# A GpSimd copy set behind the third expert addition, and an output product moved to another PSUM bank

## The reference

```
h = embed(x) * sqrt(192) + position
u = layernorm(h)
z, xBC, dt = split(rmsnorm(u) @ in_proj)        # 384, 512, 24 heads
xBC = silu(causal_conv(xBC, 4 taps) + conv_b)   # per channel, over time
state = exp(dt * A) * state + dt * x B^T        # per head, step by step
m = (state C + D x) * silu(z) @ out_proj        # the mixer
v = rmsnorm(m)
h = h + m + (silu(v @ w_gate) * (v @ w_up)) @ w_down
x = layernorm(h)
scores = sigmoid(x @ gate)                      # 8 experts in 4 groups of 2
cw = the 2 best experts of the 2 best groups, scores divided by their sum
h = h + shared expert(x) + sum over e of cw[e] * (silu(x @ w1[e]) * (x @ w3[e])) @ w2[e]
```

## Time and profile before

| | |
|---|---|
| median of 3 runs | 796.38 us (795.68 to 796.73) |
| the profiled execution | 796.69 us, of it the span of the trace 794.9 us |
| TensorE busy | 757.6 us (95%) |
| VectorE busy | 636.5 us (80%) |
| ScalarE busy | 546.8 us (69%) |
| GpSimd busy | 328.3 us (41%) |
| mean granted TensorE clock | 0.991 |

### The profile page before, as it was taken

How to read it: one execution, slowest core, us unless ns; L and a number is a source line. 1 busy time by engine, 2 the same in 40 slices (tenths; PEclk the granted TensorE clock), 3 DMA queues, 4 the chain that set the end, 5 groups by cost and what they waited for, 6 DMA issues and landing times.

```text
span 794.9 us, 23059 instructions
## 1 busy us (share of the span) xinstructions
PE 757.6 (95%) x7278; PEld 646.6 (81%) x7278; DVE 636.5 (80%) x1691; ACT 546.8 (69%) x1242; POOL 328.3 (41%) x478
## 2 busy tenths in 40 slices
PE   2679999999999999999999999999999999999897
PEld 1556788988888898888888888888988888888786
DVE  4699987879788787978878797887889788786745
ACT  4975777767777776777767677776767777675533
POOL 5355544433444443344344334434443443442222
PEclk9899999999999999999999999999999999999999
DMA  7420000000000000000000000000000000000000
GB/s 251 155 89 1 12 22 12 9 25 6 15 10 21 10 6 25 3 17 10 21 10 6 25 3 17 10 21 10 6 24 4 17 10 16 14 6 11 2 1 21
DMA packets 14923, 18.93 MB, mean 24 GB/s; under 512 B 4656, under 2 KB 13008, under 8 KB 14448
## 3 DMA queue, kind: packets, MB, share of 16 engines
q1 hardware_dynamic: 13264, 15.25, 6.0%
q0 software_dynamic: 1632, 3.34, 1.7%
HBM read 14.39 MB, written 4.19 MB: 23 GB/s over the span
## 4 chain that ended last, share of the span: by engine, by line
PE 87%; DVE 2%; issue 1%; ACT 1%; POOL 0%; DVEq 0%; POOLq 0%; ACTq 0%
PE bank L1554 40%; PE bank L1934 11%; PE bank L1862 8%; PE bank L1718 6%; PE bank L1707 5%; PE bank L1831 4%; PE bank L1818 3%; PE bank L1809 3%; PE bank L1795 2%; PE bank L1647 1%; PE bank L1652 1%; PE bank L1691 1%; DVE mr L1193 1%; PE bank L1901 0%; PE bank L1902 0%
## 5 line engine op out<-in xcount | busy, mean ns | idle before, releaser
L1193 DVE SCALAR_TENSOR_TENSOR mr<-er,gm 128x512 f32<-128x512 f32 x192 | 125.8, 692 | 4.1 <-ACT er L782 3.7
L782 ACT ACTIVATE er<-bank 128x512 f32<-128x512 f32 x192 | 106.0, 595 | 27.4 <-PE bank L1707 27.1
L1934 PE MATMUL bank<-w2t,w_raw 128*128 128x192 f32 x576 | 112.6, 327 | 0.4 <-DVE w_raw L1362 0.4
L872 ACT ACTIVATE sg<-bank 128x256 f32<-128x256 f32 x144 | 55.1, 382 | 61.8 <-PE bank L1554 50.9
L1132 DVE SCALAR_TENSOR_TENSOR xa<-xr,cw_,xa 128x256 f32<-128x256 f32 x192 | 92.4, 488 | 6.3 <-ACT xa L690 4.7
L1934 PEld LDWEIGHTS bank<-w2t,w_raw 128*128 128x128 f32 x576 | 91.0, 190 | 1.8 <-DVE w_raw L1455 0.7
L1554 PE MATMUL bank<-x_h,wt_lo 128*128 128x256 f16 x288 | 78.5, 273 | 0.0
L1554 PE MATMUL bank<-x_h,w_lo 128*128 128x256 f16 x288 | 78.5, 273 | 0.0
L1554 PE MATMUL bank<-x_l,w_hi 128*128 128x256 f16 x288 | 78.5, 272 | 0.0
L1554 PE MATMUL bank<-x_h,w_hi 128*128 128x256 f16 x288 | 78.4, 272 | 0.0
L1554 PE MATMUL bank<-x_h,wt_hi 128*128 128x256 f16 x288 | 78.4, 272 | 0.0
(11 more groups left out here) (239 smaller groups left out, 2197.3 us busy)
## 6 DMA issues: line engine op xcount, KB each, us to landing
out<-w_raw SPq DMA_DIRECT2D x16, 192.0 KB, 2.0
pos<-position SPq DMA_DIRECT2D x16, 96.0 KB, 1.9
ri<-exponent_rows SPq DMA_DIRECT2D x1, 1536.0 KB, 6.4
w_raw<-weights SPq DMA_DIRECT2D x1, 1156.0 KB, 6.0
wt_raw<-weights SPq DMA_DIRECT2D x1, 1156.0 KB, 8.4
sums<-lj SPq DMA_DIRECT2D x16, 64.0 KB, 1.9
w2t<-w SPq DMA_DIRECT2D x1, 864.0 KB, 11.6
w_raw<-weights SPq DMA_DIRECT2D x1, 768.0 KB, 8.1
```

Of the source, the lines that this page charges most:

```text
L782: act.activation(er[:, r % NER], p_d[r % 2][:].rearrange("p (h i) -> p h i", h=HG), ACT.Exp)\
L872: act.activation(sg[:, e % 4, :], src[e][:, 0:NB * Q], ACT.Silu).then_inc(sx_ready, 1)
L1193: ve.scalar_tensor_tensor(mr[:, r % NMR], er[:, r % NER], 1.0, gm[:, r // NQ, :].unsqueeze(1).to_broadcast([128, HG, Q]), ALU.min, ALU.mult)\
L1934: ins = pe.matmul(p_ex[e][:, b * D:(b + 1) * D], hh[:, e % NHH, b * Q:(b + 1) * Q], w2t[:, e, :], start=True, stop=True)
```

## The change

One edit in GpSimd's `experts`: the copy `halo(p)` stands behind the addition of e = 2 instead of behind that of e = 0, in each of the 14 passes. The other edits are all in the finale. b's two output products go to bank p_d1 instead of p_misc; the first of them stands ahead of `turn_x(a)` within `scan_back` and waits for all of b's exponentials (`e_ready`); the second stays behind gate_up(1). In exchange gate and up of a's expert 3 go to p_misc instead of p_d1 and wait for `t1_ready[1]`, and b's MLP product f = 1, which writes p_d1, waits for `hm_ready`. ScalarE's and VectorE's readers take the new bank.

```diff
-        p_gu_a = (p_pair[0], p_pair[1], p_d0, p_d1, p_pair[0], p_pair[1], p_pair[0], p_pair[1], p_pair[0])
+        p_gu_a = (p_pair[0], p_pair[1], p_d0, p_misc, p_pair[0], p_pair[1], p_pair[0], p_pair[1], p_pair[0])
...
-                    if e == 0 and p is not None:
+                    if e == 2 and p is not None:
                         halo(p)
...
-                mixed(b, p_misc)
+                mixed(b, p_d1)
                 expert_gate(a, 2, p_gu_a)
-                mixed_norm(b, p_misc)
+                mixed_norm(b, p_d1)
...
-                v_low(b, p_misc)
+                v_low(b, p_d1)
                 route_weights(a, p_gu_a)
                 hidden(a, 4, p_gu_a)
-                mixed(b, p_misc)
+                mixed(b, p_d1)
...
             def project_out(c, b, dst=p_out[0]):
-                if b == 0 and dst is p_misc:
-                    pe.wait_ge(t1_ready[1], c + 1)
+                if b == 0 and dst is p_d1:
+                    pe.wait_ge(e_ready, c * NR + NR)
...
-                scan_back(b, None, lambda: turn_x(a, None))
+
+                def turn_beside_output():
+                    project_out(b, 0, p_d1)
+                    turn_x(a, None)
+
+                scan_back(b, None, turn_beside_output)
 
                 def gate_up(e):
                     if e < 2:
                         pe.wait_ge(gt_ready, a * NF + NF - 1 + e)
+                    elif e == 3:
+                        pe.wait_ge(t1_ready[1], b + 1)
...
                     if f < 2:
                         pe.wait_ge(hh_ready, a * NX + 3 + f)
+                        if f == 1:
+                            pe.wait_ge(hm_ready, b + 1)
...
                 router(a)
                 gate_up(0)
                 gate_up(1)
-                project_out(b, 0, p_misc)
-                project_out(b, 1, p_misc)
+                project_out(b, 1, p_d1)
                 gate_up(2)
                 gate_up(3)
```

## The result

The changed kernel takes 799.65 us (median of 6 runs) beside 795.44 us for the kernel before (6 runs on the same chip): ratio 1.0049, 95% interval 1.0036 to 1.0063, so 4.2 us slower. One of the six runs lasted 979 us; it was disturbed and doesn't count in the ratio. The profiled execution has a span of 797.5 us.

A forecast was written before the change was run, and what follows sets the result against it. TensorE's row of products was taken to bound the kernel. From the median of 796.38 us, the loop adds 14 x 0.47 = 6.6 and the finale takes 1.4: forecast 801.6 us, slower by 0.65%, range 796 to 806.5.

The forecast's parts named there:

- The taps: VectorE's last convolution taps in each pass: two held by GpSimd's earlier additions, making xa 1.03 us late.
- the signs named beforehand: Trace signs of being right, among them two longest taps of 1.0 to 1.1 us in each pass.
- Rival 1: Loop's additions and taps don't hold each other; 792.3 us, faster; chance 0.13.
- The transposes: TensorE's L1647 in each pass, waiting for ScalarE's late silu L716: start 0.54 us late.
- The output product: Loop's first output product on TensorE, released 0.47 us later each pass, 6.6 us over 14 passes.
- Masked G: L1158 in each pass, waiting for ScalarE's L739: starts 1.03 us late, the weighted sums following, 0.47 late.
- the first path: TensorE's way through the late transposes and second ecx to the loop's output product: 0.4 us late.
- The finale: Kernel's end: output product moved into TensorE's pause gains 1.4 us, 0.98 by order and 0.4 by clock; bounds 0 and 2.
- The base: Time of the kernel before, from which the forecast was summed: median 796.38 us.
- Rival 2: Only one of two additions holds a tap in the loop; 795.7 us, no change that can be told; chance 0.05.
- Rival 3: ScalarE bounds the loop for the whole slip: 0.7 us or more a pass, 804.8 up to 809.4 us; chance 0.12.

The follow-up runs named there:

- e3: Kernel before with only the copy moved, behind the addition of e = 1, so one addition runs beside the taps: 795.96 us, ratio 1.0002.
- e6: Kernel before plus three products into p_d1, never read, in TensorE's pause ahead of the second norm's turn; output products unmoved: 796.00 us, ratio 0.9994.
- e11: Kernel before with only the copy moved, behind the addition of e = 3, so three additions may run beside the taps: 812.55 us, ratio 1.0214.
- e7: Loop's edit alone on the kernel before, with the additions of e = 1 and 2 replaced by one-input copies in the 14 passes: 793.72 us, ratio 0.9970.
- e9: Kernel before with the copy behind the addition of e = 1, which waits for the hidden product of expert 5: 797.03 us, ratio 1.0018.
- e2: Kernel before with the finale's edit alone, the loop's copy left behind the first addition: 794.77 us, ratio 0.9985.
- e8: Kernel before with e5's loop and e2's finale: 793.26 us, ratio 0.9960.
- e10: Kernel before with e9's loop and e2's finale: 796.13 us, ratio 1.0002.
- e4: Kernel before with the copy behind the addition of e = 2 and the addition of e = 1 waiting for xa: 794.66 us, ratio 0.9988.
- e5: Kernel before with the copy behind the addition of e = 4 and the addition of e = 1 waiting for xa: 794.90 us, ratio 0.9983.

## Why the prediction was right, and where its sizes were off

The forecast was 801.6 us, the kernel takes 799.65, within the range and on the side foreseen.

**The taps: as forecast.** Two held in each pass, by 0.62 and 0.42 for a forecast of 0.62 and 0.41; xa 1.04 late for 1.03. That came from one tap in the ramp beside one GpSimd product, carried over with its two offsets (0.85 and 0.29 there, 0.86 and 0.28 in the loop). One of the signs named beforehand was stated too narrowly: the second held tap is 0.89 us long, not 1.0 to 1.1, as it starts later in the addition that holds it; its end is where the working had it. The sentence of the Trainium skill that it was set against, Advanced Engine Details and Errata, Mode Summary, doesn't name these taps; GPSIMD Engine Reference, Specifications, names contention with two SBUF inputs, and 14 x 2 held taps agree with it. Rival 1 fell with them.

**The transposes: as forecast.** 0.54 late; the chain shows 0.16 + 0.19 + 0.19 = 0.54. The list of waits puts this wait down to "issue" and names no releaser; that it is L716 rests on the times, as L716 ends at 434.23 + 0.63 = 434.86 and the transposes begin at 435.07. I had put all of it on ScalarE's path. 0.16 of it came earlier and by another way, from the hidden product behind the first held tap to expert 7's gate and up. It changes nothing in the sum, as the transposes' release swallows it, but alone, in e3, it is the whole cost of the edit.

**The output product: the mis-sized term.** The prediction was "I take 0.47 a pass", with the wait for L1455 staying in the list. The pass is 0.38 longer and the wait is gone. Both of its paths were put too late. Masked G was to be 1.03 late and is 0.95: before, ScalarE began silu 0.12 after xa with no idle time ahead of it, now it stands idle for xa and begins 0.04 after it, so its row slips 0.08 less than xa. The weighted sums follow at 436.82 for 436.43, 0.39 late. And the first path, which the prediction has as "0.4 late", measures 0.38. The two paths end within some hundredths of each other (the product's first row takes 1.00 for 0.98), and I had taken the larger of two rough values. Which of them ends last shows in the list of waits: in the changed kernel TensorE's weight load waits for ecx (L770) in 12 places, 2.1 us in all, where the kernel before has none, and the wait for L1455 is gone. 14 x 0.47 = 6.6 us became 14 x 0.38 = 5.3.

**The finale: 1.6 for 1.4.** The order gives 1.0 (forecast 0.98) and the clock 0.6 (forecast 0.4), by e6's one trace. The product is free in the pause, the 0.76 us ahead of the MLP stays, and the half clock goes.

**The base.** The prediction stood on 796.38, three runs; six runs give 795.44. That is 0.9 of the 1.95 us by which the forecast was too high, the loop's 1.3 are most of the rest, and the finale's 0.2 goes the same way; together 2.4, and the 0.5 too much is within the interval.

**Rivals.** Rival 2 (one tap held, no change) describes e3, not this kernel. Rival 3 (0.7 us or more a pass) needs a third held tap, as in e11. Whether a GpSimd instruction must have two inputs to hold a tap is answered by e7: it needn't. What stays open is why the taps and additions keep these two distances (0.86 and 0.28); the runs show them and no cause.

## What to carry to other kernels

Before you move work of one engine to an earlier place, look at what the neighbours do there: a full-size instruction of GpSimd that reads SBUF beside VectorE instructions with two SBUF inputs made both late, and VectorE's lateness, less the slack of its readers, was the price. It can be worked out from where each instruction would end: here the held tap ends 0.28 us behind the GpSimd instruction. A wait of 0.19 us on the critical engine was removed here for 0.54 elsewhere; holding the same additions back until the last tap took less away (0.13) and kept it. In the tail, work that is ready belongs in a pause of TensorE: it came off the path and kept the clock up.

## What the runs showed of the hardware

- A full-size fp32 addition on GpSimd (128 x 384) and a two-input fp32 instruction on VectorE (128 x 256) exclude each other. The addition ends 0.86 us behind the tap that it meets, and the next tap 0.28 behind the addition; held so, a tap takes 0.89, 1.10 or 1.22 us instead of 0.48 (changed kernel, e3, e9, e11). A copy of the same size on GpSimd, with one input, does the same with the same 0.28, and as it is over sooner the tap takes 0.61 to 0.70 (e7). A VectorE instruction with one operand in PSUM isn't stretched (0.41 beside additions).
- In all eight kernels in which TensorE stood idle for 1.99 us ahead of the second norm's turn, a stretch of 3.4 us at 1.2 GHz followed; how much of it the masked products met varies (2.0 to 2.7 us for them). In the five with six matmuls in that pause and 0.67 us of it left (changed kernel, e2, e6, e8, e10) the clock stayed at 2.4 GHz and they took 1.5.
- GpSimd stands 0.15 us between two additions that follow each other. A copy of 24 columns (0.20 us) put there costs nothing: four additions take 4.44 us with it (e4) and without it (e5).
